# Attention scores as row tiles of TensorE, with four masked key copies for sixteen, in a six-stage decoder kernel

## What is computed

```python
# L0 cross attention (h = 16 heads, dk = 8)
scores = einsum('nhqd,nhkd->nhqk', q, k)
scores = where(mask == 0, -1e9, scores)
attn = softmax(scores / sqrt(dk)); out = (attn @ v) @ wo.T + bo
# L1 own attention: q = k = v = x, 16 heads
scores = einsum('bhqd,bhkd->bhqk', x, x) / sqrt(D)
# keep the u = ceil(log(129)) largest per query, softmax, @ v, out projection
# L1 cross attention: as L0's, without a mask
```

## Time and profile before

| | us |
|---|---|
| median of 3 runs | 8274.56 |
| lowest, highest | 8271.50, 8279.51 |
| profiled execution, first to last instruction (its span; no other time of it is given) | 8265.0 |
| in it: PE / PEld busy | 6420.9 / 3385.8 |
| DVE / ACT / POOL busy | 6547.0 / 4678.4 / 4871.4 |
| `mamba_stage` | about 0 to 4100 |
| `xattn_stage` | about 4116 to 4800 |
| `decoder_stage` | about 6180 to 7906 |

### The profile page before, as it was taken

One profiled execution on the slowest core, in us unless ns is written; L12 is line 12 of the kernel. 1 busy time (PEld: TensorE's weight loads), 2 busy tenths in 40 slices (PEclk: granted clock), 3 DMA queues, 4 the chain that ended last, 5 costly groups with the idle time before them and its releaser, 6 DMA issues. The chain is left out here.

```text
span 8265.0 us, 94279 instructions
## 1 busy us (share of the span) xinstructions
PE 6420.9 (78%) x25974; PEld 3385.8 (41%) x25989; DVE 6547.0 (79%) x15305; ACT 4678.4 (57%) x9323; POOL 4871.4 (59%) x2829
## 2 busy tenths in 40 slices
PE   5888888888888888888799967777547777777745
PEld 2333333333333333333355545555324544545522
DVE  5999999999999999899755568898667666666657
ACT  4666666666666666666555533333226666666633
POOL 4888888888888888888744434454223333333300
PEclk9999999999999999999899988888658988898955
DMA  5334333334333343333300057777210000000011
GB/s 185 141 152 160 141 154 153 143 152 158 143 153 152 144 155 153 145 153 153 123 26 23 20 151 213 210 211 211 79 47 6 10 10 10 10 10 10 7 33 36
DMA packets 373732, 896.59 MB, mean 108 GB/s; under 512 B 28031, under 2 KB 270076, under 8 KB 306972
## 3 DMA queue, kind: packets, MB, share of 16 engines
q1 hardware_dynamic: 332508, 692.64, 22.3%
q0 software_dynamic: 40960, 201.36, 8.6%
HBM read 850.58 MB, written 56.77 MB: 110 GB/s over the span
## 5 line engine op out<-in xcount | busy, mean ns | idle before, releaser
L365 POOL TENSOR_TENSOR mb_dBu<-mb_dtu,mb_rows_b 128x1024 f32<-128x1024 f32 x1027 | 2401.6, 2357 | 142.4 <-POOLq L63 96.2
L379 DVE TENSOR_TENSOR_SCAN mb_bank<-mb_bank,mb_dBu 128x1024 f32<-128x1024 f32 x704 | 1610.8, 2288 | 139.9 <-PEq L63 106.0
L350 ACT ACTIVATE mb_bank<-mb_dt,mb_a_neg 128x508 f32<-128x508 f32 x2050 | 1312.9, 671 | 2.3
L419 PE MATMUL mb_bank<-mb_hcd,ident 128*128 128x512 f32 x2560 | 1213.0, 607 | 30.2 <-DVE mb_hcd L393 29.7
L419 PE MATMUL mb_bank<-mb_hcp,ident 128*128 128x512 f32 x1280 | 846.1, 798 | 346.1 <-POOL mb_hcp L402 346.1
L402 POOL TENSOR_TENSOR mb_hcp<-mb_hs,mb_rows_c 128x1024 f32<-128x1024 f32 x320 | 750.9, 2346 | 478.6 <-DVE mb_hs L379 444.3
L393 DVE TENSOR_TENSOR mb_hcd<-mb_bank,mb_rows_c 128x1024 f32<-128x1024 f32 x704 | 862.1, 1225 | 32.1 <-PE mb_bank L419 0.4
L419 PEld LDWEIGHTS mb_bank<-mb_hcd,ident 128*128 128x128 f32 x2560 | 498.5, 199 | 755.6 <-issue 628.8
L1518 POOL DMA_INDIRECT ex_rows<-in_ex_table,ex_idx x512 | 489.2, 955 | 525.3 <-DVE ex_idx L1514 311.0
L379 DVE TENSOR_TENSOR_SCAN mb_hs<-mb_bank,mb_dBu 128x1024 f32<-128x1024 f32 x320 | 731.1, 2285 | 81.9 <-ACT mb_bank L350 81.9
L419 PEld LDWEIGHTS mb_bank<-mb_hcp,ident 128*128 128x128 f32 x1280 | 302.3, 251 | 776.6 <-POOL mb_hcp L402 414.3
(11 more groups left out here) (369 smaller groups left out, 13387.2 us busy)
## 6 DMA issues: line engine op xcount, KB each, us to landing
mb_rows_b<-bc_rows SPq DMA_DIRECT2D x259, 1024.0 KB, 7.5
mb_rows_c<-bc_rows SPq DMA_DIRECT2D x258, 1024.0 KB, 6.9
stream<-mb_r_post SPq DMA_DIRECT2D x69, 256.0 KB, 2.7
mb_r_tok<-stream SPq DMA_DIRECT2D x67, 256.0 KB, 2.8
mb_r_old<-stream SPq DMA_DIRECT2D x65, 256.0 KB, 2.8
ex_rows<-in_ex_table,ex_idx POOLq DMA_INDIRECT x512, 5.6
tj_x_tok<-stream SPq DMA_DIRECT2D x17, 256.0 KB, 3.0
bc_rows<-mb_xp SPq DMA_DIRECT2D x65, 64.0 KB, 1.6
```

Of the source, the lines that this page charges most:

```text
L350: e = nc.scalar.activation(da_of(n)[:, c * GB:(c + 1) * GB, 1:], dt[q][:, c].rearrange("p (b t) -> p b t", b=GB)[:, :, 1:], ACT.Exp, scale ...
L365: nc.gpsimd.tensor_tensor(by_c(dBu[m % RING][:]), by_c(chains(dtu[q][:])), over_c(rows_b[:, n]), ALU.mult).then_inc(s["mb_dbu"], 1)
L379: nc.vector.tensor_tensor_scan(flat(to), flat(da_of(n)), flat(dBu[n % RING][:]), 0.0, ALU.mult, ALU.add).then_inc(s["mb_scan"], 1)
L419: m = nc.tensor.matmul(bank[:, B_Y + c], ident[:], part[:, c * GB:(c + 1) * GB], start=False, stop=False)
```

## The change

The scores of a group of four heads no longer use all 128 rows. Four heads own 32 neighbouring channels, which is one row tile of the array. Each matmul now takes those 32 channels of the queries and of the keys, at tile position `(r, 0)`, with `r` = 0, 32, 64 or 96. Within a tile, four masked copies separate the heads, and the same four copies serve all four tiles. So `km` is 4 copies wide, and `hmask` has 4 columns, its pattern repeated every 32 partitions. The two matmuls of a unit are in different row tiles and write different banks. The mask term gets 32 rows per tile (3 with the parts of the number, 29 zeros), and its two matmuls stand behind both score matmuls, where before each stood behind its own. `left` is therefore signalled after the first mask matmul in `xattn_stage`.

```diff
-        self.km = [sb(f"{pre}_km{i}", [P, H, nk]) for i in range(2)]
+        self.km = [sb(f"{pre}_km{i}", [P, ABREAST, nk]) for i in range(2)]
...
-        self.nc.gpsimd.tensor_tensor(self.km[n % 2][:, :, 0:nk], kind.k(n % GB).unsqueeze(1).to_broadcast([P, H, nk]),
-                                     self.hmask[:].unsqueeze(2).to_broadcast([P, H, nk]), ALU.mult).then_inc(self.sem("km"), 1)
+        self.nc.gpsimd.tensor_tensor(self.km[n % 2][:, :, 0:nk], kind.k(n % GB).unsqueeze(1).to_broadcast([P, ABREAST, nk]),
+                                     self.hmask[:].unsqueeze(2).to_broadcast([P, ABREAST, nk]), ALU.mult).then_inc(self.sem("km"), 1)
...
         for j in range(2):
             if not self.topk(t - 1):
                 self.wait(pe, "shift", t - 1, less=1 - j)
-            h0 = half * HH + 4 * j
-            m = self.nc.tensor.matmul(self.scores_at(j, kind.nk), kind.q(b), self.km[n % 2][:, h0:h0 + 4, 0:kind.nk],
-                                      start=True, stop=kind.bias is None)
-            if kind.bias is not None:
-                ones3, parts = kind.bias(b)
-                m = self.nc.tensor.matmul(self.scores_at(j, kind.nk), ones3, parts.unsqueeze(1).to_broadcast([3, 4, kind.nk]),
-                                          start=False, stop=True)
-            if j == 0 and not kind.topk:
+            r = (2 * half + j) * WIDE
+            m = self.nc.tensor.matmul(self.scores_at(j, kind.nk), kind.q(b)[r:r + WIDE], self.km[n % 2][r:r + WIDE, :, 0:kind.nk],
+                                      start=True, stop=kind.bias is None, tile_position=(r, 0))
+            if j == 0 and not kind.topk and kind.bias is None:
                 m.then_inc(self.sem("left"), 1)
+        if kind.bias is not None:
+            ones, parts = kind.bias(b)
+            for j in range(2):
+                r = (2 * half + j) * WIDE
+                m = self.nc.tensor.matmul(self.scores_at(j, kind.nk), ones[r:r + WIDE],
+                                          parts[r:r + WIDE].unsqueeze(1).to_broadcast([WIDE, ABREAST, kind.nk]),
+                                          start=False, stop=True, tile_position=(r, 0))
+                if j == 0:
+                    m.then_inc(self.sem("left"), 1)
         m.then_inc(self.sem("score"), 1)
...
-        part = sb("part", [3, 1])
-        ones3 = sb("ones3", [3, P], BF16)
+        part = sb("part", [P, 1])
+        ones = sb("ones", [P, P], BF16)
...
-                            nc.vector.tensor_scalar(mbias[other][:], keep[0:3], 1.0, part[:, 0:1], ALU.subtract, ALU.mult).then_inc(p["mk"], 1)
+                            nc.vector.tensor_scalar(mbias[other][:], keep[:], 1.0, part[:, 0:1], ALU.subtract, ALU.mult).then_inc(p["mk"], 1)
```

More of the change, by code:

```diff
@@ L1204, in xattn_stage @@
         kT, qT = two("kT", [P, GB, NC]), two("qT", [P, GB, SEQ])
-        vx, mbias = two("vx", [NC, GB, H, WIDE]), two("mbias", [3, GB, NC], BF16)
+        vx, mbias = two("vx", [NC, GB, H, WIDE]), two("mbias", [P, GB, NC], BF16)
         b_res, a_res = two("b_res", [P, GB, D]), two("a_res", [P, GB, D])
@@ L1228, in kind @@
             return Kind(NC, DK ** -0.5, False, lambda b: qT[q][:, b], lambda b: kT[q][:, b], lambda b, h: vx[q][:, b, h], wo[:],
-                        add, rows_of, lambda b: (ones3[:], mbias[q][:, b]))
+                        add, rows_of, lambda b: (ones[:], mbias[q][:, b]))
         kinds = [kind(q) for q in range(2)]
@@ L1258, in _ @@
             def _(dve):
-                nc.vector.memset(ones3[:], 1.0)
+                nc.vector.memset(ones[:], 1.0)
                 for q in range(2):
@@ L1414, in xattn_host @@
             "rows": np.stack([np.asarray(i["L0_attn_normf_w"]), np.asarray(i["L0_attn_normf_b"]), A("bv"), A("bo")]),
-            "part": -bf16_parts(BIG)[:, None]}
+            "part": np.tile(np.concatenate([-bf16_parts(BIG), np.zeros(WIDE - 3, np.float32)]), P // WIDE)[:, None]}
 PH, NK, KD, EXPERTS = 8, 128, 64, 2048
@@ L2750, in build @@
         consts = {"ident": st.enter_context(nc.sbuf_tensor("ident", [P, P], F32)),
-                  "hmask": st.enter_context(nc.sbuf_tensor("hmask", [P, H], F32)),
+                  "hmask": st.enter_context(nc.sbuf_tensor("hmask", [P, ABREAST], F32)),
                   "half_neg": st.enter_context(nc.sbuf_tensor("minus_half", [P, GB], F32))}
@@ L2795 @@
             "mask": np.asarray(inputs["mask_Bx1x1xS2_ik0"]).reshape(BATCH, NC),
-            "ident": np.eye(P, dtype=np.float32), "hmask": np.repeat(np.eye(H, dtype=np.float32), DK, axis=0)}
+            "ident": np.eye(P, dtype=np.float32), "hmask": np.tile(np.repeat(np.eye(ABREAST, dtype=np.float32), DK, axis=0), (P // WIDE, 1))}
     for pre, lay in WEIGHTS.items():
```

## The result

| us | before | after |
|---|---|---|
| median | 8273.0 (4 runs, 8268.9 to 8279.5) | 8220.8 (4 runs, 8203.8 to 8243.5) |
| ratio, 95% interval | | 0.994 (0.9928 to 0.9952) |
| profiled execution, span | 8265.0 | 8201.8 |
| granted clock, whole span | 0.869 | 0.832 |
| layer 0 attention, first to last instruction | 703.9 | 686.0 |

The change makes the kernel 52 us faster, 0.6%, where 129 were forecast. Layer 0 attention gives 18 us where 94 were forecast, the decoder 44 where 32 were; the forecast had 3 more for the stages' starts. The profiled execution of after is its fastest, so its span shows 63 us of gain where the medians show 52.

The account below looks back on a forecast made before the run. PE was taken to bound layer 0 attention; in the decoder a chain through several engines, mostly DVE. Gains of 94 (layer 0), 32 (decoder) and 3 (starts) made 129 us: 8274.6 to 8146, chance 0.54, range 8080 to 8262.

Parts of the forecast that it names:

- the stages' starts: At each stage's start the first scores wait for the first keys; shorter masking saves 3 us in all.
- Layer 0, the block of scores: Layer 0 attention: score matmuls run side by side, saving 0.83 us per unit at full clock, 106 us in all.
- Rival (a): Score matmuls: passes keep their order, one in four hidden, three lengths for two; 8213 us, chance 0.12.
- no overlap: Score matmuls do not run side by side at all; about 8290 us, chance 0.04.
- Layer 0, the clock: Layer 0 attention: granted clock falls from 0.90 to 0.88, losing 12 us.
- Its own equation: Layer 0 attention: 441 us of work at clock c plus 77 idle equals the old 684 at c = 0.73.
- Rival (c): Both attention stages: TensorE falls to half clock for long, slower below about 0.77; 8382 us at 0.70; chance 0.13.
- Rival (b), ACT as the bound: Layer 0 attention: another engine becomes the bound; half the gain turns into ACT waits, 53 us lost, 8199; chance 0.17.
- Decoder, POOL's keys: Decoder: shorter key masking on POOL holds up DVE's `nb` less, saving 1.5 us per round; bounds 0 and 1.7.
- Decoder, own and cross scores: Decoder, per round: 2.6 us gained on own scores, 0.9 lost on cross scores, 1.2 lost to the clock.
- The own scores: Decoder own attention: the block falls from 1.72 to 1.08 us; 2.6 gained per round, bounds nothing and 5.3.
- the cross scores: Decoder cross attention: PE saves 0.15 us per unit, but DVE starts 0.22 later, losing 0.9 us per round.

Follow-up runs that it names:

- e2: The changed kernel, with both score matmuls of a unit reading the same 32 channels, in one row tile; 8687.1 us.
- e5: The changed kernel, with two row tiles of 64 rows instead of four of 32, and eight masked copies; 8099.9 us.
- e1: The kernel before, with only 4 masked key copies, read by every score matmul with all 128 rows (scores not the reference's); 8208.4 us.
- e7: The changed kernel, with row tiles of 64 rows, eight masked copies and extra matmuls that add no result; 8072.6 us.
- e9: The kernel before, with two small LayerNorm instructions moved ahead of the masked keys on POOL's queue in each decoder round; 8237.6 us.
- e6: The kernel before, with the 16 masked key copies made by four POOL instructions of four copies each; 8274.8 us.
- e3: The changed kernel, with extra matmuls that add no result, into an unused bank, in rounds of both attention stages; 8142.7 us.
- e10: The kernel before, with extra matmuls that add no result, into an unused bank, in rounds of both attention stages; 8245.3 us.

## Why the prediction came out as it did

**Layer 0, the block of scores: right.** The passes run two abreast (0.007 us apart; e2 takes the overlap away), the block is 0.86, and at full clock the fifth and sixth spacing of a round's units are 3.89 and 3.48 us, before 4.75 and 4.33: 0.85 saved. Rival (a), passes that keep their order, and "no overlap" fall. The rule that the prediction names for (a) isn't what falls: of the two whole matmuls the one that starts first by 0.007 us also ends first, by 0.006. What fails is the step from that rule to three lengths. PE's work came out too: busy time by clock is 587.1 x 0.757 = 444 us in the stage, and 441 were forecast. With the clock kept up a round, from its first scores to the next round's, takes the forecast 35 to 36 us: 35.2 at the median in e5, where before has 41.5 and after 39.9.

**Layer 0, the clock: wrong, the step that failed.** The prediction took 0.88 for 0.90. It stood at 0.76. Its own equation, 441 us of work at clock c plus 77 idle, gives 657 us at 0.76: 27 us gained, not 94. Measured are 18. The rest is idle time: from the stage's first instruction to its last PE is idle 686.0 - 587.1 = 98.9 us, and before 703.9 - 613.4 = 90.5. The reasons given were that PE's waits don't grow and that the score matmuls are the smaller part of its work. They speak of time and share; e5, where the clock is 0.90 and the stage 101 us shorter than before, shows that the rows of those matmuls matter with their time the same. The word "narrower" stood in the prediction, without a price. Rival (c) had the right mechanism, its sign (a clock under 0.8) is what the trace shows, and its point of turning is about right: below 0.73 and 0.79 the stages should lose. After gains a little in layer 0 at 0.76 and its tiles lose in the decoder at 0.77. Its price, 8382, was for a clock of 0.70, which didn't come; and that the time fell at all owes most to the keys (e1), not to the tiles.

**Rival (b), ACT as the bound: no.** PE waits for `pt` 67.0 us in layer 0 (4130 to 4750), before 55.3, which is far from half of the gain, and e7's round takes 33.5 us at the median with the same ACT work.

**Decoder, POOL's keys: under-costed, by 36 us.** "POOL isn't waited for" was wrong. ACT waits for L851 (the rows at e9), which stands behind the keys in POOL's queue, once a round; the wait was in the profile, only 17.1 us in the window, far down the list. The prediction counted the keys' length and what DVE suffers beside them, but not the queue. It had named it ("those are queued behind the keys and move forward"), yet priced only `nb`. e9 alone gives 2.5 us a round, e1 3.7 in the decoder; the prediction had 1.5. The 1.5 itself, for `nb`, is not confirmed by any run: in e6 `nb` shrank and the time stayed.

**Decoder, own and cross scores: the wrong sign.** The own scores on PE are as forecast, 1.13 us at full clock where the earlier trace rows has 1.88. But forecast were 2.6 - 0.9 - 1.2 = 0.5 us a round gained; against e1 the tiles cost 1.0. DVE's waits in 6220 to 7780 show it, for e1:

```profile
DVE de_a_mx L1134 <- PE de_bank L988: 82.7, 57, 3.4
DVE de_a_m L1111 <- ACT de_a_sp L1059: 76.3, 43, 7.3
DVE de_a_m L1111 <- issue: 51.9, 12, 4.6
```

and for after:

```profile
DVE de_a_mx L1140 <- PE de_bank L989: 102.9, 68, 3.8
DVE de_a_m L1117 <- issue: 66.8, 12, 5.8
DVE de_a_m L1117 <- ACT de_a_sp L1065: 55.4, 32, 5.6
```

The own scores' gain is there: DVE waits 21 us less for ACT's copies. 15 of them come back as another gap ahead of the same search, and the cross scores cost 20 (forecast 14). That leaves 14 us lost, against 16 measured. At the measured clock the formula in the prediction's rival (c), 1018/0.77 + 439 = 1761, less 1726 and counted half, gives a loss of 18 for the tiles, near the 16. This suggests the clock here too, whose fall the prediction priced at 1.2 us per round; no run isolates it for the decoder. The cross scores' block on PE is 0.72 us (1.04 before), 0.32 saved where 0.15 was forecast, so PE's side of it isn't what went wrong.

**The sum.** Of the 129 us 52 came. That 8220.8 lies in the range of 8080 to 8262 is owed to its width and to the two errors' opposite signs, 76 us too much for layer 0 attention and 12 too little for the decoder. It also lies 8 us from rival (a)'s 8213, by chance, as the passes do run abreast.

## What to carry to other kernels

Before matmuls are narrowed to row tiles, ask what the clock will be: a shorter block of fewer rows can be paid for by every other matmul of the stage. Of two tilings with the same length try the one with more rows first (here 121 us), and pad a mask or a bias with zeros to the rows of its neighbours: that alone gave 88 us of a 704 us stage. Before an engine is called unwaited-for, look through the whole list of waits for it, and at what stands behind its long instruction in its queue: reordering two small ones gave 38 us.

## What the hardware showed that was not expected

- The granted clock doesn't follow busy time: 13.00 of 13.00 us busy at 0.50, and 4.85 of 7.00 at 1.00. Over layer 0 attention PE was busy 90% of the time at 0.63 (e2), 86% at 0.76 (after) and 83% at 0.90 (e5), in part because the same work takes longer at half clock. That rows matter is shown by e5; how the chip weighs them is open.
- Work that nobody needs made a kernel faster: 78 us in e3 on the changed kernel, 30 in e10 on the kernel before. The clock over layer 0 attention rose from 0.76 to 0.87 and from 0.89 to 0.96.
- Row tiles ran two abreast though each float32 matmul is two passes, 0.79 us for four passes of 308 columns against 1.30 in one tile. How the passes of more than two tiles would interleave wasn't tried.
- The changed kernel's runs lie further apart than before's on its chip (40 us against 11; before's lay 25 apart on two other chips), at the same clock in all four (0.832 to 0.834). Why is open.
